# Layer two's chosen rows in 64 gapless tiles, worked off as 79 (tile, expert) pairs with sums kept in rings of 32

## The reference, cut to what matters

```
diff = x[:, :, None, :] - keys
logits = -sum(diff * diff, -1) + einsum('bld,ed->ble', x, rw) + rb
topv, topi = top_k(logits, 4)
w = softmax(topv, -1)
hidden = gelu(einsum('bld,efd->blef', x, w1) + b1)
exp_out = einsum('blef,edf->bled', hidden, w2) + b2
sel = take_along_axis(exp_out, topi[..., None], axis=2)
x = layernorm(x + sum(w[..., None] * sel, axis=2))
```

## Time and profile before

| what | value |
|---|---|
| time, median of 3 runs | 715.87 us |
| the profiled execution's time | 721.07 us |
| its span | 719.2 us |
| mean granted clock of PE | 0.889 |
| PE busy | 555.2 us (77%) |
| DVE busy | 486.6 us (68%) |
| ACT busy | 413.2 us (57%) |
| POOL busy | 358.7 us (50%) |
| gathers, layers one and two (line 721) | 96, 971 ns each |
| scatters of layer two (line 740) | 80, 992 ns each |
| first product's matmuls (line 1202) | 640 records, 285 ns each |
| gate scaling on ACT (line 1475) | 96, 385 ns each |

### The profile page before, as it was taken

One profiled execution on the slowest core, in us unless ns is written; L12 is line 12 of the kernel. 1 busy time (PEld: TensorE's weight loads), 2 busy tenths in 40 slices (PEclk: granted clock), 3 DMA queues, 4 the chain that ended last, 5 costly groups with the idle time before them and its releaser, 6 DMA issues.

```text
span 719.2 us, 16215 instructions
## 1 busy us (share of the span) xinstructions
PE 555.2 (77%) x4599; PEld 401.1 (56%) x4600; DVE 486.6 (68%) x1718; ACT 413.2 (57%) x1103; POOL 358.7 (50%) x463
## 2 busy tenths in 40 slices
PE   4769999998214981689999998328898888888880
PEld 2235555555103981445555555217788778878780
DVE  6788888994674424778888995866555555555437
ACT  1348888885101661648888886105566666666563
POOL 4665555405002684752333307234777777777750
PEclk9979999999555996769999999658999999999995
DMA  6502090002100136084040001033444455445463
GB/s 182 157 1 68 9 259 2 2 1 45 19 0 21 47 39 194 16 242 126 9 126 2 1 2 45 15 88 129 147 162 154 161 160 171 149 161 167 140 238 117
DMA packets 66444, 67.91 MB, mean 94 GB/s; under 512 B 17235, under 2 KB 47331, under 8 KB 65862
## 3 DMA queue, kind: packets, MB, share of 16 engines
q1 hardware_dynamic: 57846, 53.25, 23.3%
q0 software_dynamic: 8544, 13.98, 7.8%
HBM read 31.57 MB, written 13.25 MB: 62 GB/s over the span
## 4 chain that ended last, share of the span: by engine, by line
PE 41%; DVE 19%; issue 16%; DMA 9%; POOL 8%; SPq 3%; ACT 2%; DVEq 1%; POOLq 0%; ACTq 0%
PE bank L847 8%; PE bank L814 8%; PE bank L830 7%; DMA prob<-xs,idx_g 4%; POOL prob L721 4%; PE bank L1202 4%; DMA parts<-rt,idx_s 2%; DVE mx L1562 2%; DVE passed L1762 2%; POOL parts L740 2%; PE bank L1224 2%; PE bank L864 1%; DMA KB<-parts 1%; PE bank L1029 1%; PE bank L1041 1%
## 5 line engine op out<-in xcount | busy, mean ns | idle before, releaser
L1562 DVE TENSOR_REDUCE mx<-bank 128x2 f32<-128x512 f32 x256 | 166.5, 686 | 34.7 <-PE bank L814 31.7
L1312 ACT ACTIVATE prob<-bank 128x512 f32<-128x512 f32 x256 | 141.7, 597 | 47.4 <-PE bank L830 36.9
L721 POOL DMA_INDIRECT prob<-xs,idx_g x96 | 93.2, 971 | 91.3 <-DVE idx_g L1980 45.3
L1467 ACT ACTIVATE XT<-bank,prob 128x128 f32<-128x128 f32 x320 | 91.5, 368 | 51.0 <-PE bank L1202 50.0
L1224 PE MATMUL bank<-W,XT 128*128 (+1 forms) x768 | 107.7, 284 | 13.2 <-issue 11.7
L814 PE MATMUL bank<-KB,QT 128*128 128x512 f16 x256 | 100.6, 408 | 9.4 <-DVE QT L1622 3.9
L1224 PEld LDWEIGHTS bank<-W,XT 128*128 128x128 f32 x768 | 94.6, 194 | 16.8 <-issue 16.4
L740 POOL DMA_INDIRECT parts<-rt,idx_s x80 | 79.3, 992 | 28.0 <-issue 20.1
L830 PE MATMUL bank<-QT,KB 128*128 128x256 f16 x512 | 91.3, 279 | 0.0
L1202 PE MATMUL bank<-rt,prob 128*128 128x128 f32 x640 | 89.7, 285 | 0.0
L1202 PEld LDWEIGHTS bank<-rt,prob 128*128 128x128 f32 x640 | 81.5, 199 | 1.1
(11 more groups left out here) (272 smaller groups left out, 948.3 us busy)
## 6 DMA issues: line engine op xcount, KB each, us to landing
prob<-W SPq DMA_DIRECT2D x80, 258.0 KB
W<-in_w SPq DMA_DIRECT2D x48, 256.0 KB, 3.5
sum<-zero SPq DMA_DIRECT2D x3, 1024.0 KB, 9.2
xr<-XT SPq DMA_DIRECT2D x12, 128.0 KB, 2.1
xs<-X SPq DMA_DIRECT2D x2, 768.0 KB, 5.8
prob<-xs,idx_g POOLq DMA_INDIRECT x96
parts<-rt,idx_s POOLq DMA_INDIRECT x80, 2.3
XB<-sum SPq DMA_DIRECT2D x1, 1024.0 KB, 5.4
```

Source lines behind the costliest of these rows:

```text
L721: nc.gpsimd.indirect_dma_start(xg[:, q, 0:XW[lay]], None, xs[lay], bass.IndirectOffsetOnAxis(idx_g[:, q:q + 1], 0)).then_inc(gathered[q], 16)
L1312: nc.scalar.activation(prob[:, v % 8, :, :], st_bank(b, v)[:, :], ACT.Exp, scale=SCALE).then_inc(exp_done, 1)
L1467: last = nc.scalar.activation(hid[:, q, f, :], bank[2 + q % 2][:, P * f:P * f + P], (ACT.Gelu_apprx_tanh, ACT.Gelu)[lay], bias=b1)
L1562: nc.vector.tensor_reduce(m_at, bank[S1B[u % 2]][:, :].rearrange("p (j k) -> p j k", j=2), AX.X, ALU.max).then_inc(s1_used, 1)
```

## The change

The 8192 rows are no longer padded. They fill 64 tiles without gaps, and a tile may hold rows of several experts. The work is a list of 64 + 15 = 79 (tile, expert) pairs: in the order of the rows each step goes on either to the next tile or to the next expert, so pair p with expert e is on tile p - e. Each pair multiplies a whole tile with one expert's weights. A gate that is zero for rows of other experts scales the result, and DVE adds it to the tile's sum, which stays in SBUF until the tile's last possible pair is done; then the tile is scattered once.

- The list of experts by pair is packed, six to a word, into 14 words (`packed`), which PE, DVE and SP load into registers once. Expert and ring slot come from them by shift, mask and subtraction.
- Transposed tiles (`xsT2`), tile sums (`yo2`) and gates (`owned`) lie in rings of 32 tiles, gathered rows (`xg`) in a ring of 8. The rings take the place of attention buffers of the same size, which are now cut out of them.
- `turn_step` and `list_step` set in which pair's step a tile is transposed and its row list made: up to tile 31 eleven tiles in sixteen steps are waited for (tile 31 in step 21), the lists at three in two steps (tile 31 in step 16, tile 63 in step 49). Six lists come before the loop.
- POOL issues 32 gathers, then a scatter and a gather in turn 32 times, then 32 scatters. Scatter t waits for min(t + 16, 79) added pairs.
- ACT no longer scales; it clears the ring of sums once before the gate's exponentials. DVE clears a slot again when its tile is scattered.
- The stage's steps are written out; there is no hardware loop. The blank rows, four constant tables and the padding's arithmetic are gone. Layer one's stage keeps its form.

```diff
-NJT = [E0 * CAP // P, TOK * TOPK // P + E1]
+NJT = [E0 * CAP // P, TOK * TOPK // P]
+NPAIR = NJT[1] + E1 - 1
+RING, XRING = 32, 8
...
+def turn_step(t):
+
+    if t < RING:
+        return -1 if t == 0 else -((12 - 11 * t) // 16)
+    return min(t - 2, 21 - -(4 + 11 * (t - 31)) // 8)
...
+def list_step(t):
+
+    if t < 6:
+        return -1
+    return 2 * (t - 6) // 3 if t < RING else t - 14
...
+            def row_gather(t):
+
+                q = t % XRING
+                if t >= XRING:
+                    pool.wait_ge(row_turned, t - XRING + 1)
+                    pool.wait_ge(own_ready, t - XRING + 1)
+                pool.wait_ge(row_ready, t + 1)
...
+            def pair_first(words, p):
+
+                at = pair_slot(pe, words, p)
+                pe.wait_ge(rows_in, min(p + 1, NJT[1]))
+                pe.wait_ge(wc_in[p % 4], 16 * (p // 4 + 1))
+                if p >= 2:
+                    pe.wait_ge(pair_gelu, p - 1)
+                for f in range(NF):
+                    last = nc.tensor.matmul(bank[2 + p % 2][:, P * f:P * f + P], wc[:, p % 4, P * f:P * f + P],
+                                            xsT2[:, bass.ds(at, 1), :], start=True, stop=True)
...
+                for p in range(NPAIR + 2):
+                    if p < NPAIR:
+                        pair_first(words, p)
+                    for t in TURNS[p]:
+                        row_turn(t)
+                    for t in LISTS[p]:
+                        row_list_of(t)
+                    if p >= 2:
+                        pair_second(words, p - 2)
...
+            def row_listed(t):
+
+                q = t % 2
+                dve.wait_ge(row_list, t + 1)
+                nc.vector.tensor_scalar(hit[:, q, :], bank[4 + q][:, 0:P], slot_at[:, t:t + 1], bank[4 + q][:, P:P + 1],
+                                        ALU.is_le, ALU.add, accum_out=tok[:, q, :]).then_inc(lstep, 1)
+                nc.vector.tensor_copy(slot_expert[:, t:t + 1], bank[4 + q][:, P + 1:P + 2]).then_inc(lstep, 1)
+                dve.wait_ge(lstep, NJT[0] + 2 * t + 2)
+                nc.vector.tensor_copy(idx_g[:, t:t + 1], tok[:, q, :]).then_inc(row_ready, 1)
...
+            def pair_sum(words, p):
+
+                s = pair_slot(dve, words, p)
+                dve.wait_ge(pair_gate, p + 1)
+                if p == 0:
+                    dve.wait_ge(zeroed, 3)
+                else:
+                    dve.wait_ge(pair_added, p)
+                if p >= RING:
+                    dve.wait_ge(slot_clear, min(p + 1, NJT[1]) - RING)
+                dve.wait_ge(pair_out, p + 1)
+                at = yo2[:, bass.ds(s, 1), :]
+                nc.vector.scalar_tensor_tensor(out=at, in0=bank[6 + p % 2][:, 0:P].unsqueeze(1), scalar=gcol[:, p % 8:p % 8 + 1],
+                                               in1=at, op0=ALU.mult, op1=ALU.add).then_inc(pair_added, 1)
...
+                for p in range(NPAIR + 2):
+                    for t in LISTS[p]:
+                        row_listed(t)
+                    for t in LISTS[p + 1]:
+                        row_indicator(t)
+                    for t in TURNS[p]:
+                        row_owned(t)
+                    if RING <= p + 1 < NJT[1]:
+                        slot_cleared(p + 1)
+                    if p >= 2:
+                        pair_gated(words, p - 2)
+                        pair_sum(words, p - 2)
+                    if p == 3:
+                        count_tiles()
```

More of the change, by code:

```diff
@@ L1173, in slot_table, with pair_experts @@
-                last.then_inc(lo_done, 1)
+                for k in range(K):
+                    last = nc.tensor.matmul(bank[6][:, 8 + k:9 + k], before[:, :], nrow[:, k:k + 1], start=True, stop=(k == 0))
+                    if k == 1:
+                        last = nc.tensor.matmul(bank[6][:, 8 + k:9 + k], ones_b[:, :], nrow[:, 0:1], start=False, stop=True)
+                last.then_inc(lo_done, 1)
+                if lay == 0:
+                    pe.wait_ge(first_listed, 1)
+            def pair_experts():
@@ new lines, in pair_second @@
+            def pair_second(words, p):
+                e = pair_expert(pe, words, p)
+                pe.wait_ge(pair_gelu, p + 1)
+                if p >= 2:
+                    pe.wait_ge(pair_added, p - 1)
+                for f in range(NF):
+                    last = nc.tensor.matmul(slot_bank(6, p), hid2[:, p % 4, f, :],
+                                            W[:, bass.ds(e, 1), W2AT + P * f:W2AT + P * f + P], start=(f == 0),
+                                            stop=(f == NF - 1))
+                last.then_inc(pair_out, 1)
```

544 lines of the change are left out of this document (306 added, 238 removed).

## The result

The changed kernel takes 691.49 us (median of 4 runs, 690.51 to 693.01), the kernel before 715.73 beside it (4 runs, 714.72 to 717.56). The ratio is 0.964, 95% interval 0.9605 to 0.9675. The forecast was 687, range 673 to 711. The profiled execution took 691.12 us with a span of 689.3, so this one stands at its median; that of the kernel before lay 5.2 above.

What follows compares the result with a forecast made beforehand. POOL's alternating scatters and gathers (2.56 us a tile) were taken as the bound. Products ending at 664 plus a 26.4 tail gave a span of 690.4 against 719.2; 29 us off the median 715.87 made 687 us, range 673 to 711.

Steps and rivals of the forecast that it cites:

- The bound before: Layer two's expert stage: POOL sets the pace at 2.56 us a tile, TensorE behind it at 2.06.
- The stretches: Expert stage cut by turns of the pair loop; in each the slower of VectorE and TensorE counts; products end at 664.
- steps 2 to 16: Early turns of the pair loop: VectorE sets them at 45 us (38 to 52), TensorE needs 34.
- steps 17 to 49: Middle turns of the pair loop: VectorE sets them at 74 us (63 to 88), TensorE needs 68.
- steps 50 to 80: Last turns of the pair loop: TensorE sets them at 55 us, VectorE needs 31.
- VectorE's bundles: VectorE's work in the expert stage: list 0.72 us, two indicators 0.38, owned 0.38, gate and sum 0.8, clear 0.12.
- gate and sum bundle: VectorE, per pair: register instructions, wait for the gate and scaled sum, 0.6 to 1.0 us, taken as 0.8.
- The tail: Last product to end of span: third slice lands 4.6 us behind the last product, 26.4 us instead of 24.2.
- Rival 1: Expert stage: VectorE is dearer, all bundles at their high ends, 707 us; chance 0.25.
- Rival 2: Expert stage: VectorE is cheap and TensorE is the floor, 675 us; chance 0.10.
- Rival 3: Last 31 steps: gain turns into waits for weights, about 2.6 us a step, 712 us; chance 0.07.
- Rival 4: Steps 2 to 49: TensorE's clock falls to 1.2 GHz in half of them, 729 us, slower; chance 0.08.

Runs made afterwards that it cites:

- one a step: Changed kernel with one row list and one transpose in every step: 750.25 us, ratio 0.9397 to the kernel before; without scatters 687.32 us.
- the run with the short second product: Changed kernel without scatters, fourth of four matmuls of each second product left out: 693.37 us against 695.7; with scatters 747.17 us.
- with the addresses fixed: Changed kernel without scatters, VectorE's two addresses per pair replaced by constants: 689.42 us against 695.7; with scatters 748.89 us.
- the repeated run: The changed kernel itself measured once more, unedited: 751.8 us beside 798.6 of the kernel before, ratio 0.9415.

## Why the prediction was right, point by point

*The bound before.* Right: in the trace GpSimd issues with little more than its 0.30 us between two, and without scatters most tiles fall from 2.56 to the 2.06 us that the prediction had put behind it. It gives no price to what every fourth tile costs TensorE on top; the mean is 2.21. The forecast that packing saves TensorE almost nothing holds as well: 186.5 us of stage for the kernel before without scatters; the changed kernel takes 187.9 (472.9 to 660.8), and 190.3 without scatters in the same condition.

*The stretches.* Forecast against the trace: step 2 begins at 490, measured 489.1; steps 2 to 16 take 45 us, measured 46 (489.1 to the end of pair 14's sum at 535.2); steps 17 to 49 take 74, measured 72.5; steps 50 to 80 take 55, measured 53; products end at 664, measured 660.8; span 690.4, measured 689.3.

*The first of these is right by two errors, and one of them is luck.* I left the first gather at 478.1; it came at 472.9. Of the 5.2 us, 4.0 are there by the attention's last row maximum on VectorE (it starts at 430.7 before and 426.7 now), ahead of the changed stage. In the other builds of the changed kernel that instant lies between 426.1 and 432.0 and the first gather between 472.3 and 478.5, while the distance between them is 46.1 to 46.5 in every build; in the two traces of the kernel before it is 47.4 and 47.2. So 1.2 us belong to the change, and 4.0 lie within the spread between executions. The other traces have their first gather at 476.4 in the median; from there the same stage would have ended the span some 3.5 us later, 2.4 above the forecast. On the other side I wrote that three first products stand ahead of the first second product "and do so again", without asking what stands between them. From the first gather to step 2 it took 16.2 us, not 11.9. The serial start with 4.0 us a step took the gain back. The two runs with earlier transposes show the price: 2.8 us for one step earlier, 5.3 with one a step.

*VectorE's bundles.* A list costs 0.60 (0.72 forecast: the wait for the count also hides behind the copy of the expert), two indicators 0.32 to 0.33 (0.38), an owned gate 0.36 to 0.41 (0.38), the sum itself 0.35 (0.29), the clear 0.165 (0.12). The gate and sum bundle runs from 507.76 to 508.74 and costs 1.0 (0.8), the 0.41 of register work in front of it included. The high price of the last and the low price of the first cancel. The half throughput of scalar_tensor_tensor from the Trainium skill (Vector Engine (DVE) Microarchitecture Reference, section 7), estimated at 0.03 us in 32 elements, can't be settled by the 0.248 us that L2124 takes on average: a plain tensor_tensor of SBUF operands takes 0.225 at 64 elements and about 0.355 at 192, which leads down to 0.193 at 32, so 0.055 are on top, more than the rule asks for and for one shape alone.

*The tail.* Forecast 26.4, measured 28.5 (660.8 to 689.3). The third slice is issued at 662.78 and lands 7.0 us behind the last product, not 4.6. The mis-sized term is the landing of its last scatter, which I put 1 us before the last product's end. That scatter was issued in time, at 656.60, but its last event of landing is recorded at 662.70, 6.1 us later and 1.9 behind the last product. Meanwhile the first two slices, 1 MB each, were being loaded (issued at 653.53 and 654.62, there at 658.58 and 662.87). The scatter before it took 7.1 us. The median of a scatter before was 2.3. The load of the slice itself took 5.0, not 5.6.

*687 against 691.5.* The span was forecast to 1.1 us, with errors that cancel: step 2 began 0.9 early, the stretches behind it took 1.2 more, 1.5 less and 1.9 less, the tail 2.1 more. The miss comes from taking 29 us off the median, 715.87. Those 29 were worked out in an execution that lay 5.2 above that median, and the changed kernel's execution lay at its own. The difference of the medians is 24.2, that of the executions 30. Taken against its own execution, the sum was right.

*What would show it.* GpSimd's alternation gave way to waits for lists, row_turned and pair_added; TensorE waits for indicators early (7.6 and 4.4 us); pairs are 1.8 apart from step 50; the clock stays at 1.00. One sign was wrong: VectorE was to be 90% busy to 610 with idle rows that name nothing. It is 78% to 81% busy, because its register work isn't counted as busy. Someone who went by that sign would have named TensorE, 20.00 of 20 us busy, and the run with the short second product shows that this is wrong for steps 17 to 49.

*The rivals.* Rival 1 (VectorE dearer) has its mechanism but not its size. Rival 2 (TensorE is the floor) holds from step 50 and, with the addresses fixed, from step 17, as far as the lengths of the steps tell; no run has both edits. Rival 3 (weights) isn't seen: in the first trace each copy has landed 0.6 us or more before its first product starts, 1.0 or more but for the first, and 2.5 us after its issue in the median (6.0 at most). Rival 4 (the clock) didn't happen in the first trace, though TensorE was down to 18.26 of 20 us; the to and fro of the Trainium skill's page TensorE: Matmul & The Clock Gate (psum-queue depth-cycling) would have needed the clock row to leave 1.00, and from 500 us to the end of the stage it doesn't. In the runs with the late hidden layers it does (0.90 on average from 500 to 725 us of the repeated run), so its price was a real one there, behind stalls that no step of the prediction has.

## What to carry to other kernels

Count the issuing engine's queue too: a kernel with two indirect transfers per tile was held by 2.56 us of issues, and packing helped because it cut the number of issues and let rings spread them, not because it saved products. When an engine has register work in front of an instruction, its busy share understates it and a neighbour's full busy share may mean nothing; shorten each by a known amount and see which one moves the end. And a saving from two single executions is taken off the profiled execution's own time, and only then compared with medians.

## What the runs showed of the hardware

In the changed kernel's trace VectorE mostly stands still for 0.33 to 0.42 us in front of the gate's copy, for its register instructions, when a reduction of 0.17 us is the last instruction before them, for 0.20 to 0.28 behind the reduction and a clear, and for 0.14 behind the reduction and a fill of 0.27 (508.28 to 508.43). So they run on while another instruction works.

In the condition of eleven runs the engines that read TensorE's results went on late after their recorded end, by up to 6.2 us in the repeated run and 13.7 in another, and in the stall shown both readers did at nearly the same moment. Most of it came once scatters to memory had begun, but nine hidden layers were late without any. The kernel before lost 74 to 83 us in this condition and the changed kernel 60, part of it probably by the lower clock that is seen behind stalls. Without scatters the changed kernel lost 4; the kernel before has one late hidden layer then (0.8 us), and no run of it in the normal condition to compare with. The copies of the weights landed no later than in the first trace (a median of 2.3 us after their issue against 2.5), which speaks against the bandwidth of transfers, though only 436 of the 1264 events of landing are recorded in that trace. What holds the readers up stays open. It makes a kernel with fewer scatters better off by more (0.9415 against 0.964), for a reason that no step of the prediction has.
